# A selective scan with both channel halves of a step as one scan of 1024 columns and one product by C

## What is computed

```
A = -exp(A_log);  dt = softplus(...);  B, C = projections of x
h[t] = exp(dt[t] * A[d, n]) * h[t-1] + dt[t] * B[t, n] * x[t, d]
y[t, d] = sum over n of h[t] * C[t, n]  + D[d] * x[t, d]
```

## Time and profile before

| | |
|---|---|
| median of 3 runs | 718.21 us (717.24 to 718.5) |
| span of the profiled execution | 713.3 us |
| around the span, against the median | 4.9 us |
| mean granted TensorE clock | 0.949 |
| busy share PE, DVE, ACT, POOL | 90%, 76%, 74%, 62% |
| first PE matmul of scan 0 and of scan 1 | 55.71, 307.37 us |
| end of POOL's last product in scan 0 | 220.58 us |

### The profile page before, as it was taken

How to read it: one execution, slowest core, us unless ns; L and a number is a source line. 1 busy time by engine, 2 the same in 40 slices (tenths; PEclk the granted TensorE clock), 3 DMA queues, 4 the chain that set the end, 5 groups by cost and what they waited for, 6 DMA issues and landing times.

```text
span 713.3 us, 13062 instructions
## 1 busy us (share of the span) xinstructions
PE 640.6 (90%) x4408; PEld 550.0 (77%) x4409; DVE 542.7 (76%) x1030; ACT 526.5 (74%) x1295; POOL 443.4 (62%) x396
## 2 busy tenths in 40 slices
PE   4758999999994759489999999989999999999995
PEld 2348999999994423389999999988677777777684
DVE  6897999999998795969999999996932644434316
ACT  2959999999996969699999999975543562222224
POOL 0036999999998250359999999991575134333400
PEclk9959999999997869679999999999999999999998
DMA  6032555544450000134535454544123233333173
GB/s 185 7 72 80 147 143 141 145 141 143 141 149 1 0 0 6 26 98 147 159 130 155 135 149 142 147 141 151 59 97 110 74 104 105 108 105 106 55 244 118
DMA packets 57579, 77.86 MB, mean 109 GB/s; under 512 B 8112, under 2 KB 38480, under 8 KB 57520
## 3 DMA queue, kind: packets, MB, share of 16 engines
q1 hardware_dynamic: 53728, 66.75, 32.0%
q0 software_dynamic: 3792, 10.36, 4.1%
HBM read 58.21 MB, written 18.87 MB: 108 GB/s over the span
## 4 chain that ended last, share of the span: by engine, by line
PE 77%; DVE 10%; ACT 10%; issue 1%; POOL 1%; DMA 1%; ACTq 0%; DVEq 0%
PE bank L1153 25%; PE bank L1176 15%; PE bank L1221 12%; PE bank L1155 4%; ACT tok_a L771 3%; PE bank L1229 3%; PE bank L1230 3%; PE bank L1172 2%; PE bank L1066 2%; DVE st L373 2%; DVE arena L471 1%; PE bank L1323 1%; PE bank L1297 1%; PE bank L1289 1%; PE bank L1092 1%
## 5 line engine op out<-in xcount | busy, mean ns | idle before, releaser
L976 POOL TENSOR_TENSOR arena<-arena,rings 128x512 f32<-128x512 f32 x256 | 317.6, 1284 | 21.6 <-DVE arena L574 20.5
L574 DVE TENSOR_TENSOR_SCAN arena<-rings,bank 128x512 f32<-128x512 f32 x256 | 300.1, 1208 | 15.1 <-PE bank L1155 7.5
L1153 PE MATMUL bank<-rings,tok_a 128*128 128x128 f32 x1536 | 216.9, 278 | 4.7 <-ACT rings L868 4.7
L1153 PEld LDWEIGHTS bank<-rings,tok_a 128*128 128x128 f32 x1536 | 195.4, 195 | 5.3 <-issue 5.3
L878 ACT ACTIVATE rings<-arena,a_sb 128x512 f32<-128x512 f32 x256 | 170.1, 715 | 0.4 <-DVE arena L574 0.4
L1176 PE MATMUL bank<-ident,arena 128*128 128x128 f32 x1024 | 152.4, 273 | 1.1 <-POOL arena L976 1.1
L868 ACT ACTIVATE rings<-ident,b_tok 128x128 f32<-128x128 f32 x384 | 125.3, 393 | 0.4 <-ACT tok_a L833 0.4
L1176 PEld LDWEIGHTS bank<-ident,arena 128*128 128x128 f32 x1024 | 119.4, 141 | 1.9 <-POOL arena L976 1.8
L1016 POOL DMA_INDIRECT y_tok<-rings,dest x47 | 44.9, 955 | 85.1 <-DVE rings L715 84.8
L1155 PE MATMUL bank<-ident,rings 128*128 128x128 f32 x256 | 70.7, 276 | 0.0
L950 ACT ACTIVATE silu<-bank 128x176 f32<-128x176 f32 x47 | 14.9, 317 | 73.4 <-PE bank L1221 73.4
(11 more groups left out here) (179 smaller groups left out, 942.0 us busy)
## 6 DMA issues: line engine op xcount, KB each, us to landing
rings<-c_rows SPq DMA_DIRECT2D x128, 256.0 KB, 3.4
w_sb<-w SPq DMA_DIRECT2D x18, 352.0 KB, 4.3
x_sorted<-zeros SPq DMA_DIRECT2D x47, 128.0 KB, 3.4
rings<-x_sorted SPq DMA_DIRECT2D x47, 128.0 KB, 2.0
arena<-w SPq DMA_DIRECT2D x2, 2048.0 KB, 12.7
residual<-x SPq DMA_DIRECT2D x4, 512.0 KB, 5.8
tok_a<-y_tok SPq DMA_DIRECT2D x4, 512.0 KB, 7.5
w_sb<-y_tok SPq DMA_DIRECT2D x4, 512.0 KB, 8.4
```

What stands on the lines that cost most here:

```text
L574: dve.tensor_tensor_scan(state[:, u % STATE_RING, :], abar[:, u % ABAR_RING, :], bank[u % B_RING][:, :], 0.0, ALU.mult, ALU.add).then_inc( ...
L976: pool.tensor_tensor(s, s, crep[:, k % CREP_RING, :], ALU.mult).then_inc(hc_ready, 1)
L1153: pe.matmul(o, tok_a[:, c, h * P:(h + 1) * P], v_ring[:, s % V_RING, j, 0:P], start=True, stop=True)
```

## The change

Both halves of a step become one unit. The scan runs over 1024 columns that lie side by side. So that the second half doesn't go on from the state of the first, its first column of dt is set to 1e30 after u = dt * x has been computed: exp(a * 1e30) is 0 there, because a is kept at or below -1e-25. POOL writes that column once per layer. The product is one instruction of 1024 columns whose C row is repeated by an outer stride of zero. PE issues the inputs of both halves, then the sums of both. Rings hold the same bytes: 4 states, 2 decays and 2 inputs, now of whole steps; the sum comes 3 steps later, as before. ACT still computes two decays of 512 columns, but waits once for both.

```
-STATE_RING, ABAR_RING, CREP_RING, V_RING, B_RING = 8, 4, 4, 4, 4
+STATE_RING, ABAR_RING, CREP_RING, V_RING, B_RING = 4, 2, 4, 4, 2
+LEAST_RATE, LONG_STEP = 1e-25, 1e30
-SUM_LAG = 6
+SUM_LAG = 3
...
+        both = [ctx.enter_context(nc.psum_tensor(f"both{i}", [P, H * SEQ], F32)) for i in range(B_RING)]
+        bank = [both[i // H][:, i % H * SEQ:(i % H + 1) * SEQ] for i in range(H * B_RING)]
...
-                dve.tensor_scalar(a_sb[l][:, :, :], a_sb[l][:, :, :], -1.0, None, ALU.mult).then_inc(a_ready, 1)
+                dve.tensor_scalar(a_sb[l][:, :, :], a_sb[l][:, :, :], -1.0, -LEAST_RATE, ALU.mult, ALU.min).then_inc(a_ready, 1)
...
                 for s in range(STEPS):
-                    for h in range(H):
-                        u = s * H + h
-                        dve.wait_ge(b_ready, base + u + 1)
-                        dve.wait_ge(abar_ready, base + u + 1)
-                        if u >= STATE_RING:
-                            dve.wait_ge(state_free, base + u + 1 - STATE_RING)
-                        dve.tensor_tensor_scan(state[:, u % STATE_RING, :], abar[:, u % ABAR_RING, :], bank[u % B_RING][:, :],
-                                               0.0, ALU.mult, ALU.add).then_inc(h_ready, 1)
+                    dve.wait_ge(b_ready, base + s + 1)
+                    dve.wait_ge(abar_ready, H * (base + s + 1))
+                    if s >= STATE_RING:
+                        dve.wait_ge(state_free, base + s + 1 - STATE_RING)
+                    dve.tensor_tensor_scan(state[:, s % STATE_RING, :], abar[:, s % ABAR_RING, :], both[s % B_RING][:, :],
+                                           0.0, ALU.mult, ALU.add).then_inc(h_ready, 1)
...
-                    for h in range(H):
-                        u = s * H + h
-                        if u >= ABAR_RING:
-                            act.wait_ge(h_ready, base + u + 1 - ABAR_RING)
-                        act.activation(abar[:, u % ABAR_RING, :], dtT[:, h, b * SEQ:(b + 1) * SEQ], ACT.Exp,
+                    if s >= ABAR_RING:
+                        act.wait_ge(h_ready, base + s + 1 - ABAR_RING)
+                    for h in range(H):
+                        act.activation(abar[:, s % ABAR_RING, h * SEQ:(h + 1) * SEQ], dtT[:, h, b * SEQ:(b + 1) * SEQ], ACT.Exp,
                                        scale=a_sb[l][:, h, n:n + 1]).then_inc(abar_ready, 1)
...
+                act.wait_ge(edge_ready, l + 1)
...
+                for s in range(STEPS):
+                    pool.wait_ge(crep_loaded[s % CREP_RING], 16 * (l * STEPS // CREP_RING + s // CREP_RING + 1))
+                    pool.wait_ge(h_ready, l * STEPS + s + 1)
+                    h_both = state[:, s % STATE_RING, :].rearrange("p (h t) -> p h t", h=H)
+                    c_row = crep[:, s % CREP_RING, :].unsqueeze(1).to_broadcast([P, H, SEQ])
+                    pool.tensor_tensor(h_both, h_both, c_row, ALU.mult).then_inc(hc_ready, 1)
...
+                    if q == Q - 1:
+                        pool.wait_ge(u_ready, k + 1)
+                        firsts = dtT[:, H - 1, :].rearrange("p (b t) -> p b t", b=BATCH)[:, :, 0:1]
+                        pool.memset(firsts, LONG_STEP).then_inc(edge_ready, 1)
...
+                def inputs(s):
+
+                    pe.wait_ge(v_ready, base + s + 1)
+                    if s >= B_RING:
+                        pe.wait_ge(h_ready, base + s + 1 - B_RING)
+                    for h in range(H):
+                        for j in range(CQ):
...
+                    pe.wait_ge(hc_ready, base + s + 1)
+                    for h in range(H):
                         for j in range(CQ):
...
+                for s in range(STEPS):
+                    inputs(s)
+                    if s >= SUM_LAG:
+                        total(s - SUM_LAG)
```

More of the change, by code:

```diff
@@ L559, in scan @@
                 settle()
-                base = l * BATCH * UNITS
+                base = l * STEPS
                 for q in range(Q):
@@ L1138, in scan @@
             def scan(l):
[L1140 to L1155, removed]
+                base = l * STEPS
+                def inputs(s):
[4 more added lines that the diff above has]
+                        for j in range(CQ):
+                            o = both[s % B_RING][:, h * SEQ + j * P:h * SEQ + (j + 1) * P]
+                            if j < DIAGONAL:
+                                c = s // N * CQ + j
+                                pe.matmul(o, tok_a[:, c, h * P:(h + 1) * P], v_ring[:, s % V_RING, j, 0:P], start=True, stop=True)
+                            else:
+                                ins = pe.transpose(o, v_ring[:, s % V_RING, j, h * P:(h + 1) * P], ident[:, :])
                     ins.then_inc(b_ready, 1)
@@ L1160, in y_part, with total @@
                     return ysum_of[b % 2][j // 2][:, (j % 2 * H + h) * P:(j % 2 * H + h + 1) * P]
-                def total(u):
-                    b, n, h = u // UNITS, u % UNITS // H, u % H
-                    if n == 0 and h == 0 and b >= 2:
+                def total(s):
+                    b, n = s // N, s % N
+                    if n == 0 and b >= 2:
                         pe.wait_ge(ysum_free, (l * (BATCH - 1) + b - 1) * H)
@@ L1168, in total @@
                         if b == 0:
-                            pe.wait_ge(d_ready, l * H + h + 1)
-                        for j in range(CQ):
-                            c = b * CQ + j
-                            pe.matmul(y_part(b, j, h), feat_a[:, h, c * P:(c + 1) * P], d_diag[:, h, :],
-                                      start=h == 0 and j % 2 == 0, stop=False, skip_group_check=True)
-                    pe.wait_ge(hc_ready, base + u + 1)
-                    for j in range(CQ):
-                        ins = pe.matmul(y_part(b, j, h), state[:, u % STATE_RING, j * P:(j + 1) * P], ident[:, :], start=False,
-                                        stop=n == N - 1, is_transpose=True, skip_group_check=True)
+                            pe.wait_ge(d_ready, (l + 1) * H)
+                        for h in range(H):
+                            for j in range(CQ):
+                                c = b * CQ + j
+                                pe.matmul(y_part(b, j, h), feat_a[:, h, c * P:(c + 1) * P], d_diag[:, h, :],
+                                          start=h == 0 and j % 2 == 0, stop=False, skip_group_check=True)
+                    pe.wait_ge(hc_ready, base + s + 1)
+                    for h in range(H):
+                        for j in range(CQ):
+                            ins = pe.matmul(y_part(b, j, h), state[:, s % STATE_RING, h * SEQ + j * P:h * SEQ + (j + 1) * P],
+                                            ident[:, :], start=False, stop=n == N - 1, is_transpose=True, skip_group_check=True)
                     ins.then_inc(state_free, 1)
@@ L1183, in scan @@
                 pe.wait_ge(utr_copied, (l + 1) * Q * 2)
-                for u in range(BATCH * UNITS):
-                    inputs(u)
-                    if u >= SUM_LAG:
-                        total(u - SUM_LAG)
-                for u in range(BATCH * UNITS - SUM_LAG, BATCH * UNITS):
-                    total(u)
+                for s in range(STEPS):
+                    inputs(s)
+                    if s >= SUM_LAG:
+                        total(s - SUM_LAG)
+                for s in range(STEPS - SUM_LAG, STEPS):
+                    total(s)
             def weight_turns():
```

29 lines of the change are left out of this document (10 added, 19 removed).

## The result

The changed kernel takes 720.63 us (median of 7 runs, 718.92 to 721.45) against 717.78 for the kernel before in the same comparison (7 runs): ratio 1.0046, 95% interval 1.003 to 1.0062, so 3.3 us slower (0.0046 x 717.78; 2.2 to 4.5 by the interval). The direction and the range of the prediction hold.

A forecast was written before the change was run, and what follows sets the result against it. PE, issuing without a gap, was taken to bound the scan's body. Per layer, fill +0.9, order -0.44, scan +1.04 and product +0.48 made +2.0; two layers, +4.0 on 718.21, gave 722.2 us, range 719.9 to 727.0.

The forecast's parts named there:

- What bounds the kernel: Scan body: PE issues 22 records a step without a gap and sets 40.7 us per batch row; gain 0 there.
- ring margin of 0.85 us: B ring in the body: scan(s) ends 0.85 us before inputs(s+2) need it, so PE's queue stays full.
- Rival (c): Body loses its margin through a slower product or scan, making PE wait: 724 to 728, or 731; chance 0.2.
- The sizes: Instructions of 1024 columns: DVE's scan taken as 2.26 us, POOL's product as 2.32 per step, lasting 2.37.
- The fill: Start of each layer's scan: inputs(3) wait for scan(1), so inputs(4) come later, +0.9 us per layer.
- The order: End of each layer's scan: one total of 0.44 us stands behind PE's last inputs and not between, -0.44 per layer.
- POOL's end therefore decides when the next stage begins: Drain: POOL's last product ends 2.0 us later per layer, and the next stage starts 2.0 later with it.
- The terms of the scan and of the product: Drain, per layer: the longer last scan adds 1.04 us and the longer last product 0.48.
- rival (b): Drain: the first shift (L388) slips in ahead of POOL's last product, 0.9 us less per layer: 720.4; chance 0.17.
- product(62): Drain: POOL's product before the last, forecast to end about when the first shift is issued, so that shift could pass.
- Saved fixed cost makes it faster: Rival: DVE and POOL save 0.1 to 0.14 us a step, at most 0.6 per layer: 717.0; chance 0.03.
- rival (d): Granted clock: later start gains, 717.5, chance 0.08; second case, clock falls in last drain, +6 us, 728, chance 0.04.

The follow-up runs named there:

- fill_split: The changed kernel with the first four steps of a layer by halves (inputs, scan and product): 717.89 us, ratio 1.0015 to the kernel before.
- inputs_joined: The kernel before with only PE's order joined (inputs of both halves, then both sums), scans and products by halves: ratio 0.9995.
- two_shifts: The kernel before with the first two shifts behind a scan computed by four one-column, one-tensor-input operations each: 736.56 us, ratio 1.0169.
- two_shifts_early: As two_shifts, with the third group of normalisings also ordered ahead of the last batch row's statistics: 736.3 us, ratio 1.0162.

## Why the prediction was right and where it wasn't

- **What bounds the kernel: right.** PE's 22 records per step set 40.7 us per batch row, and 40.69 came back in every row. The saving of DVE and POOL, 23 us of busy time, gave nothing there. The ring margin of 0.85 us that I worried about held: no PE wait in the body. Rival (c) didn't happen; from where it would wasn't tried.
- **The sizes: right.** Scan 2.29 us (2.26 taken), product 2.37 (2.37). The 2.37 was summed from contiguous rows, so the outer stride of zero of the C row shows no cost of its own; no run has the contiguous product of 1024 to compare.
- **The fill: right, a little small.** +0.9 predicted, +1.1 measured. (In the prediction's sum scan(1) should end at 60.65 + 2.26 = 62.91, not 62.95, which makes +0.85.) The forecast's wait of 0.95 to 1.0 appeared as 0.68 and 0.91 of idle time. fill_split shows it to be DVE's scan(1) and worth 2.2 us in all.
- **The order: right.** -0.44 predicted, -0.43 and -0.44 measured. What inputs_joined adds: PE's order alone moves the last scan by only 0.08, because the last half scan then waits for the one ahead of it. The 0.44 belongs to the order and the joined scan together.
- **The step that failed**, though the time stayed in the range, is "POOL's end therefore decides when the next stage begins", carried over to the changed kernel. It made +2.0 per layer; measured 1.5. The terms of the scan and of the product are there: from the last scan's start the product ends 1.54 us later than before, for 1.04 + 0.48 = 1.52 predicted. But the first shift passes ahead of that product, and the chain goes round it. This is rival (b), with a chance of 0.17 and priced at 0.9 per layer; it gave back 0.7. With that and the fill of 1.1 the sum is 2 x (2.0 + 0.2 - 0.7) = +3.0, for 3.3 timed. What I should have weighed more is my own arithmetic: product(62) was to end about when the shift is issued. The two came 0.05 us apart or less, and an order that hangs on so little deserved a chance near the forecast's own. The total of 722.2 was 1.6 us above the measured 720.63; the range held because (b) had been priced and put inside it.
- **"Saved fixed cost makes it faster": refuted here.** In busy time the joined scan saves 0.07 us a step (8.4 us over 128) and the joined product 0.11 (14.7 over 128); by single durations the scan saves 0.15 (2.29 for twice 1.22), part of which back-to-back halves save already by overlapping. The Trainium skill (Advanced Engine Details and Errata, The Read-Write Bubble) advises large tiles to save such overhead on VectorE and ScalarE. For the scan on DVE the saving is in the trace, and the kernel is slower all the same, since PE sets the rate of the body and the fill and the drain grow.
- **The clock**, rival (d): the timed 3.3 us are met by the terms without it, so neither of its two cases shows. It did double the difference between the two profiled spans. In two_shifts and two_shifts_early, though, its second case showed itself: PE waited in the drain of scan 1 and the clock fell behind it.

## What to carry to other kernels

When one engine is saturated through a stage, larger instructions on the others can't shorten its body; they lengthen its fill (the ring turns over in larger pieces, so the saturated engine waits) and its drain. Join only what doesn't stand between the last input and the next stage, and take the first and the last steps apart. Where a small operation of an engine takes ten times its usual time, find what it ends with; then, before you take that wait away, work out what the other engine will do with the time, because it may run through and hold up the next one, and a longer wait there can cost TensorE its clock as well.

## What was not expected of the hardware

- A DVE instruction with two tensor inputs in SBUF (the shift, 4 columns, 0.16 us) is held while POOL runs tensor_tensor instructions, and ends some 0.02 us after one of them. Often that isn't the first one: it took 1.95 us over two products, 2.96 over three, 2.79 over five additions, 6.04 over the last product and eight additions. In other places it ended with the first one, though the next followed without a pause: 2.14 us with the changed kernel's last product (224.50 for 224.48, additions from 224.44), and 0.32 between two additions of the same trace. What decides between the two isn't shown. The reciprocals and the one-column operations with one tensor input, issued among the same products, took 0.15 to 0.22 us each.
- Behind 2.62 and 4.12 us of idle TensorE in the drain of scan 1 the granted clock fell to 0.50 for 6.8 and 10.2 us of its work (two_shifts, two_shifts_early). The idle times of 1.12 and 0.48 us at that place in the kernel before were followed by none.
- The stretch at half clock that lies over the start of a scan lasted 3.41 to 6.17 us in these profiles, and moves a fill by half of that difference: 1.4 us over the two fills here, of 3.2 that the clock put between the two profiled spans. The stages have to be compared at equal clock, or the timed runs decide.
